# Three pairs of PSUM banks for the radial products of a graph convolution, and row numbers of the gather kept in SBUF

## The chip, the cores and the metric

The kernel runs on one core of a Trainium2 chip. The metric is the device time of one execution in microseconds (us), as the median of several runs. Lower is better. The engines are named as in the profile: PE is TensorE's matrix multiply and PEld its weight load, DVE is VectorE, ACT is ScalarE, POOL is GpSimd, SP is SyncE, which only issues DMAs here.

## The reference

A graph of 12,500 nodes with 32 features has 200,000 edges, sorted by destination. Twelve message-passing layers (the first network, `L0`) come first; the change doesn't touch them. Then comes one equivariant convolution (`L1`), and its output is added to the features:

```python
h = jnp.maximum(_layernorm(x, axis=-1), 0.0)
x = x + _L1_gnn_ref(h, edge_weight, edge_attr_3, edge_index, w1, b1, w2, b2)
```

For each edge the convolution computes a hidden layer of 64 values from one distance (`relu(d * w1 + b1)`), multiplies it with `w2` to radial weights, multiplies those with the source node's features and with spherical harmonics of the edge's direction (`einsum('euv,ef,evi,ofi->euo', Rb[..., k], Yf, Fb, C)`), and adds the 32 resulting values into the edge's destination node. The kernel folds the 320 radial weights per edge into 448 columns.

## The kernel before, in words

The edges have been sorted into slots: a tile is one slot for each of 125 lanes, a unit is 20 tiles (`UNIT_TILES`), and there are 100 units. Each slot has a record of 14 words in DRAM (`slots`): the number of the source row, the lane, the weight and the local frame. The convolution works in turns of two units, so in 50 turns (`UNIT_PAIRS`) of 40 tiles. A turn is cut into five groups of eight tiles (`PAIR_GROUPS`, `GROUP`), and a group into four pairs of tiles (`GROUP_PAIRS`). DVE does one `group_step` per group; I call it a step. A short loop behind the main one (the overflow turns, `Over`) does the same for the edges that found no slot, in three turns of three groups; there the sums of half tiles are added node by node.

All engines run in program order and meet through semaphores. The parts that matter:

- **PE**, `radial_pair` (L1893 to L1903): for each pair, two bias multiplications (L1898) and two fp32 ones (L1901) fill two PSUM banks, one per tile. Banks 0 to 3 make two pairs of banks (`radial = banks(0, QUAD)`). A pair may be filled when DVE has multiplied the pair before the last (`radial_used`), and when ACT has the hidden layer of its four tiles ready (`hidden_ready`). Behind the four pairs' products come 24 small matmuls (`add_group`, L1922), which add the group's messages into two more banks (`conv_sums`).
- **DVE**, `group_step` (L1356 on): `multiply` for pair 0 and 1 (L1347 and L1351 each read the pair's banks), `project` for the next group (three instructions at L1320, which need the gathered rows), `multiply` for pair 2, the reduction L1330, `multiply` for pair 3, `project_plus` (L1336), then reductions and products (L1376 to L1401) that end in the group's messages.
- **ACT**: `main_marks` (L1583, L1588), `main_small` (the hidden layer, L1567), `main_scalars` (L1605, eight features of each gathered row), in an order written out by hand (`pair_step`).
- **SP**: `load_rec` (L655) loads the records of half a turn, once DVE has signalled `unit_done` for the half (behind L1394 of group 2 and of group 4) and POOL `unit_claimed`.
- **POOL**: `gather_unit` (L766 on) waits for `unit_done` and for the records, then issues 20 indirect DMAs (L772), each of which gathers 125 rows of `feature_table` by the row numbers that stand in the records.

Before the graph layers, ten pieces of the records pass through SBUF (`pieces`), and DVE copies three of their columns out (L1076 to L1078); between them it waits for the next load.

Of the kernel before, what the change touches and what calls it, by code (L numbers as in the profile page):

```python
# [24 lines left out]
def build_gnn(nc, x, src, dst, edge_attr, edge_weight, lift_W, lift_b, proj_W, proj_b, w1, b1, w2, b2, out):  # L25
# [99 lines left out]
    assert PAIR_GROUPS * GROUP == 2 * UNIT_TILES and PAIR_GROUPS == 5  # L125
    BUFFER_OF = (0, 1, 0, 1, 2)
    CHUNK_PAIRS = STEPS // 2
    UNIT_PAIRS = UNITS // 2
# [33 lines left out]
    with ctx:  # L162
# [164 lines left out]
        spill_marks = carve(SPILL_RING * SPILL_BATCH * LANES // 2).bitcast(BF16).rearrange("p (t n) -> p t n", n=LANES)  # L327
        hgT = carve(2, BANK)
        lane_gap = message_words[:, 0:MARKED_BY_ACT * LANES // 2].bitcast(BF16).rearrange("p (t n) -> p t n", n=LANES)

# [50 lines left out]
        gathered_rows = hg_words[:, 1024:1024 + 2 * UNIT_TILES * D].rearrange("p (s t d) -> p s t d", s=2, d=D)  # L381
        rec_tiles = rec.rearrange("p s t w -> p (s t) w")
        row_tiles = gathered_rows.rearrange("p s t d -> p (s t) d")
        spill_dist = hgT[0:SPILL_PART, 0, 0:LANES]
# [21 lines left out]
        turned, outs = banks(4, 2), banks(0, 4)  # L406
        radial, conv_sums, half_sums = banks(0, QUAD), banks(4, 2), banks(4, 4)
        spill_dist_psum = psum[0:SPILL_PART, 7 * BANK + 256:7 * BANK + 256 + LANES]
# [99 lines left out]
        rec_loaded = [sem(f"rec_loaded{s}") for s in range(2)]  # L508
        unit_claimed = [sem(f"unit_claimed{s}") for s in range(2)]
        unit_done = [sem(f"unit_done{s}") for s in range(2)]  # L510
# [26 lines left out]
        def _(sp):  # L537
# [128 lines left out]
            with sp.Fori(0, UNIT_PAIRS, 1) as i:  # L666
                for half in range(2):
                    sp.wait_ge(unit_done[half], i + 1)
                    sp.wait_ge(unit_claimed[half], i + 1)
                    load_rec(half, i)  # L670
# [7 lines left out]
        def _(pool):  # L678
# [87 lines left out]
            def gather_unit(half, i):  # L766
                pool.wait_ge(features_stored, 16)
                pool.wait_ge(unit_done[half], i + 1)
                pool.wait_ge(rec_loaded[half], 16 * i + 16)
                claim(7 + half, unit_claimed[half])  # L770
                for t in range(UNIT_TILES):
                    g.indirect_dma_start(out=gathered_rows[0:SLOTS, half, t, :], out_offset=None, in_=feature_table,  # L772
                                         in_offset=bass.IndirectOffsetOnAxis(
                                             ap=rec[0:SLOTS, half, t, 0:1].bitcast(I32), axis=0)
                                         ).then_inc(rows_gathered[half * QUADS + t // QUAD], 16)
# [22 lines left out]
        def _(dve):  # L798
# [16 lines left out]
            for s in range(2):  # L815
                v.engine_nop().then_inc(unit_claimed[s], 1)
                v.engine_nop().then_inc(unit_done[s], 1)
# [255 lines left out]
            for k in range(PIECES):  # L1073
                at = slice(k * PIECE, (k + 1) * PIECE)
                dve.wait_ge(slots_loaded[k % 2], 16 * (k // 2) + 16)
                v.tensor_copy(slot_lane[0:SLOTS, at], pieces[0:SLOTS, k % 2, :, 1])  # L1076
                v.tensor_copy(slot_w[0:SLOTS, at], pieces[0:SLOTS, k % 2, :, 2])
                v.tensor_copy(slot_src[0:SLOTS, at], pieces[0:SLOTS, k % 2, :, 3]).then_inc(slots_read, 1)  # L1078
            dve.wait_ge(src_psum_ready, 1)
# [220 lines left out]
            class Main:  # L1300
                chain, groups, first_group, first_turn = conv_step, PAIR_GROUPS, 0, 0
                row_of, rec_of = row_tiles, rec_tiles

            class Over:
                chain, groups, first_group, first_turn = over_step, SPILL_GROUPS, MAIN_GROUPS, UNIT_PAIRS
                row_of, rec_of = spill_rows, spill_rec

            def frames_of(kind, g):
# [34 lines left out]
            def multiply(kind, nth, g, pair):  # L1343
                at, bank = slice(2 * pair, 2 * pair + 2), slice(2 * (pair % 2), 2 * (pair % 2) + 2)
                z = inputs_of(g)[:, at, :, :]
# [10 lines left out]
            def group_step(kind, i, g, ahead):  # L1356
# [16 lines left out]
                if ahead:  # L1373
                    plus = project_plus(kind, nxt, summed)
                dve.wait_ge(radial_used, GROUP_PAIRS * nth + GROUP_PAIRS + 2)
                vectors = chain.mark(v.tensor_reduce(  # L1376
# [94 lines left out]
        def _(act):  # L1471
# [127 lines left out]
            def main_scalars(i, g):  # L1599
# [77 lines left out]
        def _(pe):  # L1677
# [215 lines left out]

            def radial_pair(nth, slot, pair):
                pe.wait_ge(hidden_ready, nth + 1)
                pe.wait_ge(radial_used, 2 * nth + pair + 1)
                for odd in range(2):
                    mm(radial[:, 2 * pair + odd, 0:MIX_S + MIX_V], ones_bf[odd * HIDDEN:odd * HIDDEN + PARTS, :],  # L1898
                       bias_bf[odd * HIDDEN:odd * HIDDEN + PARTS, :], start=True, stop=False)
                for odd in range(2):  # L1900
                    last = mm(radial[:, 2 * pair + odd, 0:MIX_S + MIX_V],  # L1901
                              hidden[odd * HIDDEN:(odd + 1) * HIDDEN, slot, pair * LANES:(pair + 1) * LANES],
                              w2_mix[odd * HIDDEN:(odd + 1) * HIDDEN, :], start=False, stop=True)  # L1903
                last.then_inc(radial_ready, 1)

            def first_quad(group):
                for pair in range(2):
                    radial_pair(2 * group, 0, pair)

            def second_quad(group):  # L1910
                for pair in range(2):
                    radial_pair(2 * group + 1, 1, pair)

# [18 lines left out]

            first_quad(0)
            with pe.Fori(0, CHUNKS - 1, 1) as j:
                clear_conv_sums(j)
                with pe.Fori(0, CHUNK_PAIRS, 1) as m:
                    for g in range(PAIR_GROUPS):
                        nth = (j * CHUNK_PAIRS + m) * PAIR_GROUPS + g
                        second_quad(nth)
                        first_quad(nth + 1)  # L1940
                        add_group(nth, g)
            clear_conv_sums(CHUNKS - 1)
            with pe.Fori((CHUNKS - 1) * CHUNK_PAIRS, UNIT_PAIRS - 1, 1) as m:
                for g in range(PAIR_GROUPS):
                    second_quad(m * PAIR_GROUPS + g)
                    first_quad(m * PAIR_GROUPS + g + 1)
                    add_group(m * PAIR_GROUPS + g, g)
            for g in range(PAIR_GROUPS):
                nth = (UNIT_PAIRS - 1) * PAIR_GROUPS + g
                second_quad(nth)  # L1950
                if g + 1 < PAIR_GROUPS:
                    first_quad(nth + 1)
                add_group(nth, g)
# [14 lines left out]

            turns = pe.value_load(conv_turns[0:1, 0:1], min_val=1, max_val=MAX_SPILL_TURNS * SPILL_PARTS)
            with pe.Fori(0, turns, 1) as i:  # L1970
                pe.wait_ge(conv_loaded, 16 * i + 16)
                nc.tensor.transpose(spill_dist_psum, spill_rec[:, 0:SPILL_PART, 2], identity[:, :]
                                    ).then_inc(spill_turned_ready, 1)
                first_quad(i * SPILL_GROUPS + MAIN_GROUPS)
                for g in range(SPILL_GROUPS):
                    nth = i * SPILL_GROUPS + g + MAIN_GROUPS
                    second_quad(nth)
                    if g + 1 < SPILL_GROUPS:
                        first_quad(nth + 1)
                    add_over(nth, g)  # L1980
# [23 lines left out]
```

## Time and profile before

| | us |
|---|---|
| median of 3 runs | 11822.15 (11821.74 to 11833.75) |
| the profiled execution, its own time | 11825.35 |
| its span, first to last instruction | 11823.7 |
| start of the convolution's first step | 8035.76 |
| end of the 50 turns, the last chunk's sums begin to be moved | 11559.04 |
| mean granted TensorE clock | 0.791 |

Everything up to about 8000 us is the sorting and the twelve layers; from there to the end is the convolution. Times of the trace are counted from the span's start. An idle time in brackets stands before the instruction of its row, with the instruction whose end released it.

### The profile page before, as it was taken

How to read it: one execution, taken by the hardware profiler on the slowest of the kernel's cores; microseconds unless marked ns; L12 is line 12 of the kernel's file. 1: busy time of each engine (PE TensorE's matmuls, PEld its weight loads, DVE VectorE, ACT ScalarE, POOL GpSimd, SP SyncE). 2: the span in 40 equal slices, each digit the busy share in tenths (PEclk: the TensorE clock that was granted, in tenths of full speed). 3: DMA queues.
4: the chain of work that ended last, by engine and by line, in shares of the span. 5: the costliest groups of instructions: out<-in, count | busy, mean ns of one | idle time of the engine just before them, and what ended most of it. 6: DMA issues, size and time to landing. Idle time of an engine off the chain costs nothing.

```text
span 11823.7 us, 340699 instructions
## 1 busy us (share of the span) xinstructions
PE 7408.7 (63%) x130038; PEld 4971.8 (42%) x130039; DVE 9354.8 (79%) x19079; ACT 3124.7 (26%) x7571; POOL 5296.6 (45%) x5027
## 2 busy tenths in 40 slices
PE   2555555200877877777777787775666666666663
PEld 2444444100766666666666676661222222222221
DVE  8777777457777877777777777778999999999995
ACT  0111111057222222222222222223333333333331
POOL 3777777400321221231131122116667766676773
PEclk9999999965988988888898898885555555555555
DMA  4111111067745754654564575551111111111111
GB/s 168 26 25 26 26 25 26 27 233 272 205 146 148 208 150 150 177 166 148 163 189 148 161 208 162 160 151 37 34 32 33 32 31 34 32 33 32 31 32 19
DMA packets 718056, 1212.33 MB, mean 103 GB/s; under 512 B 186449, under 2 KB 334068, under 8 KB 713636
## 3 DMA queue, kind: packets, MB, share of 16 engines
q1 hardware_dynamic: 434084, 1058.42, 28.6%
q0 software_dynamic: 146832, 69.31, 5.7%
q10 hardware_dynamic: 136012, 67.95, 2.4%
q8 instruction: 907, 14.86, 0.5%
q14 instruction: 221, 1.80, 0.1%
HBM read 1050.89 MB, written 140.94 MB: 101 GB/s over the span
## 4 chain that ended last, share of the span: by engine, by line
PE 37%; DVE 18%; issue 18%; DMA 4%; POOL 3%; DVEq 1%; ACT 1%; SPq 0%; POOLq 0%; ACTq 0%
PE psum L1814 9%; PE psum L1782 9%; PE psum L1901 7%; PE psum L1797 6%; DVE space L1383 2%; DVE space L1351 2%; PE psum L1898 2%; DMA space<-src_rows 2%; POOL space L772 2%; PE psum L1859 2%; DVE space L1387 1%; PE psum L1886 1%; DVE space L1394 1%; DMA space<-slots 1%; PE psum L1870 1%
## 5 line engine op out<-in xcount | busy, mean ns | idle before, releaser
L772 POOL DMA_INDIRECT space<-feature_table,space x2000 | 2430.5, 1215 | 598.3 <-issue 587.9
L700 POOL TENSOR_TENSOR claim_out<-claim_in 128x1 f32<-128x1 f32 x443 | 108.3, 245 | 5072.1 <-DMA table<-space 2639.0
L1901 PE MATMUL psum<-w_mix,space 64*128 64x448 f32 x4144 | 1818.2, 974 | 0.0
L1532 ACT ACTIVATE space<-psum 128x375 f32<-128x375 f32 x2400 | 955.1, 436 | 3006.7 <-PE psum L1782 2963.9
L709 POOL DMA_INDIRECT slots<-space x1568 | 1506.7, 961 | 466.1 <-issue 412.8
L1137 DVE TENSOR_TENSOR space<-psum,space 128x320 f32<-128x320 f32 x2400 | 1069.0, 486 | 786.1 <-PE psum L1797 715.6
L1782 PE MATMUL psum<-space 128*32 128x125 fp8e4 x72000 | 1341.1, 224 | 255.8 <-issue 253.2
L1814 PE MATMUL psum<-space 128*128 128x96 bf16 x24000 | 1292.6, 207 | 235.4 <-issue 146.2
L1782 PEld LDWEIGHTS psum<-space 128*32 128x32 bf16 x72000 | 1079.2, 98 | 509.8 <-issue 504.5
L1814 PEld LDWEIGHTS psum<-space 128*128 128x128 fp8e4 x24000 | 1105.3, 97 | 391.3 <-issue 270.9
L755 POOL DMA_INDIRECT space<-table,space x864 | 1099.4, 1272 | 280.9 <-issue 280.9
L1143 DVE TENSOR_TENSOR space<-space 128x320 f32<-128x320 f32 x2400 | 1062.6, 485 | 35.7 <-issue 35.7
L1147 DVE TENSOR_TENSOR space<-space 128x320 f32<-128x320 f32 x2400 | 1069.5, 487 | 0.0
L1797 PE MATMUL psum<-identity,space 128*128 128x128 f32 x6000 | 906.6, 283 | 109.4 <-ACT space L1532 41.0
L1347 DVE TENSOR_TENSOR space<-psum,space 128x512 f32<-128x512 f32 x1036 | 711.9, 687 | 261.1 <-PE psum L1901 250.6
L1922 PE MATMUL psum<-space 128*128 128x32 bf16 x6000 | 200.4, 188 | 1090.9 <-DVE space L1401 1090.9
L1722 PE MATMUL psum<-space 128*128 128x100 bf16 x1568 | 295.3, 278 | 824.0 <-DVE space L942 688.8
L1922 PEld LDWEIGHTS psum<-space 128*128 128x128 bf16 x6000 | 180.8, 104 | 1369.6 <-issue 1336.5
L1797 PEld LDWEIGHTS psum<-identity,space 128*128 128x128 f32 x6000 | 655.0, 143 | 139.0 <-issue 79.4
L1583 ACT ACTIVATE space<-columns,space 128x128 bf16<-128x128 f32 x2072 | 656.1, 387 | 198.6 <-issue 178.2
L1567 ACT ACTIVATE space<-space,b_col,w_col 128x256 f32<-128x256 f32 x518 | 309.4, 598 | 1359.7 <-PE psum L1901 1350.2
L1898 PE MATMUL psum<-space,ones_bf 3*128 3x448 bf16 x2072 | 548.9, 527 | 187.9 <-DVE space L1351 112.6
(289 smaller groups left out, 11803.5 us busy)
## 6 DMA issues: line engine op xcount, KB each, us to landing
space<-marks SPq DMA_DIRECT2D x2400, 320.0 KB
space<-src_rows SPq DMA_DIRECT2D x102, 640.0 KB, 4.7
marks<-space SPq DMA_DIRECT2D x100, 640.0 KB, 3.2
space<-distances ACTq DMA_DIRECT2D x200, 320.0 KB, 4.8
space<-block_ids SPq DMA_DIRECT2D x198, 200.0 KB
slots<-space SPq DMA_DIRECT2D x83, 448.0 KB, 9.1
space<-feature_table,space POOLq DMA_INDIRECT x2072, 2.7
slots<-space POOLq DMA_INDIRECT x1608, 2.1
```

Source lines behind the costliest of these rows:

```text
L709: g.indirect_dma_start(out=slots, out_offset=bass.IndirectOffsetOnAxis(ap=stage_row[:, s, c:c + 1], axis=0), in_=stage[:, s, c, :], in_off ...
L755: g.indirect_dma_start(out=spill_rows[0:GATHERED, t, :], out_offset=None, in_=table, in_offset=bass.IndirectOffsetOnAxis(ap=spill_rec[0:GA ...
L772: g.indirect_dma_start(out=gathered_rows[0:SLOTS, half, t, :], out_offset=None, in_=feature_table, in_offset=bass.IndirectOffsetOnAxis(ap= ...
L1137: v.tensor_tensor(row[:, half, :], slots_of_unit[:, half, :], slot_w[:, bass.ds(at * UNIT_TILES + k * HALF_TILES, HALF_TILES)].rearrange(" ...
L1143: v.tensor_tensor(left[:, half, :], row[:, half, :], tops[0][:, half, :], ALU.subtract).then_inc(left_split, 1)
L1147: v.tensor_tensor(least[:, half, :], left[:, half, :], tops[1][:, half, :], ALU.subtract).then_inc(least_split, 1)
L1532: a.activation(to[:, s0:s1, :, :], pair_picked[:, bank, 0:(s1 - s0) * PICK_COLS].rearrange("p (k c r) -> p k c r", k=s1 - s0, r=CAP), ACT.Copy
L1782: last = mm(pair_picked[D * g:D * (g + 1), bank, (s - s0) * PICK_COLS:(s - s0 + 1) * PICK_COLS], parts[:, q * SRC_PER_TILE + s, c, :], cel ...
L1797: last = nc.tensor.transpose(slots_of_unit[:, c * LANE_GROUPS:(c + 1) * LANE_GROUPS, :].rearrange("p t d -> p (t d)"), picked[:, q % 2, c, ...
L1814: last = mm(unit_sums[:, t // SUMS_PER_BANK, to:to + PARTS * D], mark_ring[:, q % RING, 1, t * LANES:(t + 1) * LANES], message_halves[:, q ...
L1898: mm(radial[:, 2 * pair + odd, 0:MIX_S + MIX_V], ones_bf[odd * HIDDEN:odd * HIDDEN + PARTS, :], bias_bf[odd * HIDDEN:odd * HIDDEN + PARTS, ...
L1901: last = mm(radial[:, 2 * pair + odd, 0:MIX_S + MIX_V], hidden[odd * HIDDEN:(odd + 1) * HIDDEN, slot, pair * LANES:(pair + 1) * LANES], w2 ...
```

## The change

The radial products get three pairs of banks (0 to 5) and the message sums move to banks 6 and 7. Pair number n of a turn (0 to 19) uses the banks n mod 3. PE now fills pair 3 of a group and then pairs 0, 1 and 2 of the next, before it adds the group. In the overflow turns two pairs are used in the old order, and PE's first transposition there waits until the sums have been moved.

The row numbers are copied out of the pieces early (a fourth DVE copy for each of ten pieces, into `slot_row`). During the convolution ACT copies 20 of them per half turn into `row_index` (`copy_index`), and the gathers read them there. They wait for that copy and for a new signal, `rows_projected`, which DVE gives in step 1 and in step 3 when the last reader of the half's rows has run, and no longer for `unit_done` and the records. SP's load of records no longer waits for POOL.

```diff
+    TURN_PAIRS = PAIR_GROUPS * GROUP_PAIRS
+    RADIAL_PAIRS = 3
...
+        slot_row = carve(SLOT_TILES).bitcast(I32)
...
+        row_index = hg_words[:, 1024 + 2 * UNIT_TILES * D:1024 + 2 * UNIT_TILES * (D + 1)].bitcast(I32).rearrange(
+            "p (s t) -> p s t", s=2)
...
-        radial, conv_sums, half_sums = banks(0, QUAD), banks(4, 2), banks(4, 4)
+        radial, conv_sums, half_sums = banks(0, 2 * RADIAL_PAIRS), banks(6, 2), banks(4, 4)
...
                     sp.wait_ge(unit_done[half], i + 1)
-                    sp.wait_ge(unit_claimed[half], i + 1)
                     load_rec(half, i)
...
             def gather_unit(half, i):
                 pool.wait_ge(features_stored, 16)
-                pool.wait_ge(unit_done[half], i + 1)
-                pool.wait_ge(rec_loaded[half], 16 * i + 16)
-                claim(7 + half, unit_claimed[half])
+                pool.wait_ge(index_copied, 2 * i + half + 1)
+                pool.wait_ge(rows_projected, 2 * i + half + 1)
+                pool.wait_ge(scatter_claimed[half], i + TURNS // 2)
+                claim(7 + half, scatter_claimed[half])
...
-                                             ap=rec[0:SLOTS, half, t, 0:1].bitcast(I32), axis=0)
+                                             ap=row_index[0:SLOTS, half, t:t + 1], axis=0)
...
+                v.tensor_copy(slot_row[0:SLOTS, at], pieces.bitcast(I32)[0:SLOTS, k % 2, :, 0])
...
+                def ring_of(g, pair):
+                    return (g * GROUP_PAIRS + pair) % RADIAL_PAIRS
...
             def multiply(kind, nth, g, pair):
-                at, bank = slice(2 * pair, 2 * pair + 2), slice(2 * (pair % 2), 2 * (pair % 2) + 2)
+                at, ring = slice(2 * pair, 2 * pair + 2), kind.ring_of(g, pair)
+                bank = slice(2 * ring, 2 * ring + 2)
...
                     plus = project_plus(kind, nxt, summed)
+                if ahead and kind is Main and nxt in (2, 4):
+                    v.engine_nop().then_inc(rows_projected, 1)
...
+            def copy_index(i, half):
+                if not (isinstance(i, int) and i == 0):
+                    act.wait_ge(rows_gathered[(half + 1) * QUADS - 1], 16 * QUAD * i)
+                    act.wait_ge(scalars_copied, PAIR_GROUPS * i - 2 + 2 * half)
+                a.activation(row_index[0:SLOTS, half, :],
+                             slot_row[0:SLOTS, bass.ds((2 * i + half) * UNIT_TILES, UNIT_TILES)],
+                             ACT.Copy).then_inc(index_copied, 1)
...
+                    if q8 in (2, 6) and not last:
+                        copy_index(i + 1, q8 // 4)
...
+            act.wait_ge(rec_cleared, 4)
+            for half in range(2):
+                copy_index(0, half)
...
-            def radial_pair(nth, slot, pair):
-                pe.wait_ge(hidden_ready, nth + 1)
-                pe.wait_ge(radial_used, 2 * nth + pair + 1)
+            def radial_pair(group, pair, ring, held):
+                slot, upper = divmod(pair, 2)
+                pe.wait_ge(hidden_ready, 2 * group + slot + 1)
+                pe.wait_ge(radial_used, GROUP_PAIRS * group + pair + 3 - held)
...
+            def main_pair(group, g, pair):
+                at = (g * GROUP_PAIRS + pair) % TURN_PAIRS
+                radial_pair(group, pair, at % RADIAL_PAIRS, 2 if at < 2 else RADIAL_PAIRS)
+
+            def over_pair(group, pair):
+                radial_pair(group, pair, pair % 2, 2)
...
                         nth = (j * CHUNK_PAIRS + m) * PAIR_GROUPS + g
-                        second_quad(nth)
-                        first_quad(nth + 1)
+                        main_pair(nth, g, 3)
+                        for pair in range(3):
+                            main_pair(nth + 1, g + 1, pair)
                         add_group(nth, g)
...
             turns = pe.value_load(conv_turns[0:1, 0:1], min_val=1, max_val=MAX_SPILL_TURNS * SPILL_PARTS)
+            pe.wait_ge(sums_moved, CHUNKS + 1)
```

## Rows read from the trace of the kernel before

**Rows 1.** The page: busy time of each engine; DVE's busy tenths in 40 slices.
```profile
PE 7408.7 (63%) x130038; PEld 4971.8 (42%) x130039; DVE 9354.8 (79%) x19079; ACT 3124.7 (26%) x7571; POOL 5296.6 (45%) x5027
...
DVE  8777777457777877777777777778999999999995
```

**Rows 2.** Busy by stretch: length, PE, PEld, DVE, ACT, POOL, TensorE clock, DMA, GB/s.
```profile
9000.00:9600.00 600.00, 404.44 (x2042) 129.92 (x2040) 545.80 (x982) 222.06 (x552) 421.95 (x361) 0.57 0.19 32
```

**Rows 3.** Waits of DVE, 8035 to 11558 us: total, times, longest.
```profile
DVE space L1347 <- PE psum L1901: 228.1, 448, 1.5
DVE space L1320 <- DMA space<-feature_table,space: 35.8, 50, 7.0
DVE space L1347 <- issue: 8.0, 38, 0.3
```

**Rows 4.** DVE in one step, in order of time: start, length, instruction, idle before.
```profile
9321.45 0.68 DVE L1347 TENSOR_TENSOR space<-psum,space 128x512 f32<-128x512 f32 x1
...
9323.58 0.88 DVE L1320 TENSOR_TENSOR space<-space 128x192 f32<-128x192 f32 x3
...
9325.05 0.69 DVE L1347 TENSOR_TENSOR space<-psum,space 128x512 f32<-128x512 f32 x1 [0.59 <-PE psum L1901]
...
9326.13 0.74 DVE L1330 TENSOR_REDUCE space<-space 128x192 f32<-128x576 f32 x1
...
9327.33 0.69 DVE L1347 TENSOR_TENSOR space<-psum,space 128x512 f32<-128x512 f32 x1 [0.46 <-PE psum L1901]
...
9328.54 1.74 DVE L1376 TENSOR_REDUCE space<-space 128x192 f32<-128x1536 f32 x1
...
9335.39 0.68 DVE L1347 TENSOR_TENSOR space<-psum,space 128x512 f32<-128x512 f32 x1
```

**Rows 5.** DVE in the first turn, a pair 3 whose products were there.
```profile
8046.89 0.74 DVE L1330 TENSOR_REDUCE space<-space 128x192 f32<-128x576 f32 x1
8047.55 0.68 DVE L1347 TENSOR_TENSOR space<-psum,space 128x512 f32<-128x512 f32 x1
```

**Rows 6.** PE in the step of rows 4, in order of time.
```profile
9321.68 0.80 PE L1922 MATMUL psum<-space 128*128 128x32 bf16 x24 [5.04 <-DVE space L1401]
...
9322.66 0.55 PE L1898 MATMUL psum<-space,ones_bf 3*128 3x448 bf16 x2 [0.17 <-DVE space L1351]
...
9323.14 1.86 PE L1901 MATMUL psum<-w_mix,space 64*128 64x448 f32 x4
...
9324.94 0.55 PE L1898 MATMUL psum<-space,ones_bf 3*128 3x448 bf16 x2
```

**Rows 7.** POOL by line, 8100 to 11500 us: busy, mean ns, idle before.
```profile
L772 POOL DMA_INDIRECT space<-feature_table,space x1937 | 2353.5, 1215 | 579.4 <-issue 569.1 <-DMA space<-slots 10.4
L700 POOL TENSOR_TENSOR claim_out<-claim_in 128x1 f32<-128x1 f32 x97 | 23.0, 237 | 446.6 <-DMA space<-slots 445.3
```

**Rows 8.** The convolution's start in order of time; last the store's time to landing.
```profile
8005.16 0.33 SPq L659 DMA_DIRECT2D feature_table<-space  x1
...
8014.23 0.85 SPq L655 DMA_DIRECT2D space<-slots  x2
...
8019.57 1.21 POOL L772 DMA_INDIRECT space<-feature_table,space  x1 [0.17 <-issue]
...
8031.62 1.20 POOL L772 DMA_INDIRECT space<-feature_table,space  x1 [0.30 <-issue]
...
8032.85 0.93 DVE L1320 TENSOR_TENSOR space<-space 128x192 f32<-128x192 f32 x3 [21.22 <-DMA space<-feature_table,space]
...
feature_table<-space SPq DMA_DIRECT2D x1, 1664.0 KB, 5.3
```

**Rows 9.** DVE between the pieces of the records, one of eight such waits.
```profile
2374.69 0.33 DVE L1076 COPY space<-space 125x200 f32<-125x200 f32 x1 [9.67 <-DMA space<-slots]
```

**Rows 10.** The first overflow turn's start: PE's transposition and ACT's copy.
```profile
11559.29 0.39 PE L1972 MATMUL psum<-identity,space 128*24 128x128 f32 x1 [0.29 <-issue]
...
11560.10 0.27 ACT L1636 ACTIVATE space<-psum 24x128 f32<-24x128 f32 x1 [21.55 <-DVE xs L1413]
```

More of the change, by code:

```diff
@@ L508, in build_gnn @@
         rec_loaded = [sem(f"rec_loaded{s}") for s in range(2)]
-        unit_claimed = [sem(f"unit_claimed{s}") for s in range(2)]
+        index_copied = sem("index_copied")
+        rows_projected = sem("rows_projected")
         unit_done = [sem(f"unit_done{s}") for s in range(2)]
@@ L815, in _ @@
             for s in range(2):
-                v.engine_nop().then_inc(unit_claimed[s], 1)
+                v.engine_nop().then_inc(rows_projected, 1)
                 v.engine_nop().then_inc(unit_done[s], 1)
@@ L1306, in _, with ring_of @@
                 row_of, rec_of = spill_rows, spill_rec
+                def ring_of(g, pair):
+                    return pair % 2
             def frames_of(kind, g):
@@ L1374, in group_step @@
                     plus = project_plus(kind, nxt, summed)
+                if ahead and kind is Main and nxt in (2, 4):
+                    v.engine_nop().then_inc(rows_projected, 1)
                 dve.wait_ge(radial_used, GROUP_PAIRS * nth + GROUP_PAIRS + 2)
@@ L1892, in _ @@
             pe.wait_ge(weights_spread, 16 * 3)
-            def radial_pair(nth, slot, pair):
-                pe.wait_ge(hidden_ready, nth + 1)
-                pe.wait_ge(radial_used, 2 * nth + pair + 1)
+            def radial_pair(group, pair, ring, held):
+                slot, upper = divmod(pair, 2)
+                pe.wait_ge(hidden_ready, 2 * group + slot + 1)
+                pe.wait_ge(radial_used, GROUP_PAIRS * group + pair + 3 - held)
                 for odd in range(2):
-                    mm(radial[:, 2 * pair + odd, 0:MIX_S + MIX_V], ones_bf[odd * HIDDEN:odd * HIDDEN + PARTS, :],
+                    mm(radial[:, 2 * ring + odd, 0:MIX_S + MIX_V], ones_bf[odd * HIDDEN:odd * HIDDEN + PARTS, :],
                        bias_bf[odd * HIDDEN:odd * HIDDEN + PARTS, :], start=True, stop=False)
                 for odd in range(2):
-                    last = mm(radial[:, 2 * pair + odd, 0:MIX_S + MIX_V],
-                              hidden[odd * HIDDEN:(odd + 1) * HIDDEN, slot, pair * LANES:(pair + 1) * LANES],
+                    last = mm(radial[:, 2 * ring + odd, 0:MIX_S + MIX_V],
+                              hidden[odd * HIDDEN:(odd + 1) * HIDDEN, slot, upper * LANES:(upper + 1) * LANES],
                               w2_mix[odd * HIDDEN:(odd + 1) * HIDDEN, :], start=False, stop=True)
                 last.then_inc(radial_ready, 1)
[L1906 to L1912, printed above, removed]
+            def main_pair(group, g, pair):
[3 more added lines that the diff above has]
+                radial_pair(group, pair, pair % 2, 2)
             def add_group(nth, g):
@@ L1931, in clear_conv_sums @@
                        start=True, stop=True)
-            first_quad(0)
+            for pair in range(3):
+                main_pair(0, 0, pair)
             with pe.Fori(0, CHUNKS - 1, 1) as j:
@@ L1938, in _ @@
                         nth = (j * CHUNK_PAIRS + m) * PAIR_GROUPS + g
-                        second_quad(nth)
-                        first_quad(nth + 1)
+                        main_pair(nth, g, 3)
+                        for pair in range(3):
+                            main_pair(nth + 1, g + 1, pair)
                         add_group(nth, g)
@@ L1944, in _ @@
                 for g in range(PAIR_GROUPS):
-                    second_quad(m * PAIR_GROUPS + g)
-                    first_quad(m * PAIR_GROUPS + g + 1)
-                    add_group(m * PAIR_GROUPS + g, g)
+                    nth = m * PAIR_GROUPS + g
+                    main_pair(nth, g, 3)
+                    for pair in range(3):
+                        main_pair(nth + 1, g + 1, pair)
+                    add_group(nth, g)
             for g in range(PAIR_GROUPS):
                 nth = (UNIT_PAIRS - 1) * PAIR_GROUPS + g
-                second_quad(nth)
+                main_pair(nth, g, 3)
                 if g + 1 < PAIR_GROUPS:
-                    first_quad(nth + 1)
+                    for pair in range(3):
+                        main_pair(nth + 1, g + 1, pair)
                 add_group(nth, g)
@@ L1973, in _ @@
                                     ).then_inc(spill_turned_ready, 1)
-                first_quad(i * SPILL_GROUPS + MAIN_GROUPS)
+                for pair in range(2):
+                    over_pair(i * SPILL_GROUPS + MAIN_GROUPS, pair)
                 for g in range(SPILL_GROUPS):
                     nth = i * SPILL_GROUPS + g + MAIN_GROUPS
-                    second_quad(nth)
+                    for pair in range(2, GROUP_PAIRS):
+                        over_pair(nth, pair)
                     if g + 1 < SPILL_GROUPS:
-                        first_quad(nth + 1)
+                        for pair in range(2):
+                            over_pair(nth + 1, pair)
                     add_over(nth, g)
```

## The prediction

> **What bounds the kernel now.** I began with the page. No engine fills the span, and the page's table in 40 slices shows that the share of the whole says little: DVE's digit is mostly 7 in the layers and 9 in the slices of the convolution [rows 1]. The table by stretches gives the number for 600 us in its middle: DVE works 545.80 of 600 us, POOL 422, PE 404, ACT 222, and the granted TensorE clock is 0.57 of full, near the lower of its two levels, 1.2 GHz [rows 2]. So the most that a change of waiting can win there is DVE's remaining 9%. I then asked who DVE waits for in the 50 turns: 228.1 us in 448 waits for radial products, 35.8 us in 50 waits for gathered rows, 8.0 us at the edges of its own loop [rows 3]. The last column of that view matters too: one of the 50 waits for rows is 7.0 us long, so the other 49 have 28.8 us, 0.59 each.
>
> Then one step in order of time [rows 4]. It lasts from 9321.45 to 9335.39, 13.94 us. Pairs 0 and 1 run without a gap; DVE then projects, waits 0.59 us for pair 2 and 0.46 us for pair 3. The same stretch on PE [rows 6] shows the reason: PE starts pair 2 at 9322.66, when DVE's L1351 on pair 0 has just ended, and needs 9324.94 - 9322.66 = 2.28 us for a pair; DVE goes on at 9325.05, 2.39 us after PE's start. There are two pairs of banks, so this wait is for a bank, not for PE's throughput: four pairs and the additions are 4 x 2.28 + 0.80 = 9.9 us of a 13.94 us step. Nine waits in a turn of ten products is right too: the wait for rows, once a turn, covers one.
>
> **The products.** With three pairs of banks, pair 2 is filled in the step before. Pair 3 starts when pair 0 is used, at about 1.2 us into the step (today's 9322.66 - 9321.45), and is ready at 1.21 + 2.39 = 3.6 us. DVE wants it without any wait at 9327.33 - 9321.45 - 0.59 - 0.46 less two overlaps (below), 4.7 us. That is 1.1 us of slack. The next group's pairs 0 to 2 follow on PE at about 5.9, 8.2 and 10.5 us, and DVE wants them at 12.7 us and later; at a turn's edge, where the ring of three restarts, pair 0 waits for pair 2's use and the chain ends near 11.1 us. The additions come behind them and wait for the messages, as now. ACT's hidden layer for the later pairs is released by pair 3's products at 3.6 us and takes 0.6 us, so it is there before PE comes to it. Thus both waits go.
>
> A wait costs more than its length, since neighbours on DVE overlap. After L1330, which takes 0.74 us, pair 3 starts 0.66 us later where its products are there [rows 5] and 1.20 us later where they aren't [rows 4]: 0.54 us gained for a wait of 0.46. So the products give 228.1 + 448 x 0.08 = 263.9 us. The step becomes 13.94 - 1.05 - 0.16 = 12.73 us, and a turn, now (11559.04 - 8035.76) / 50 = 70.5 us with its loop edge and its share of the moved sums, loses 5.3 us.
>
> **The gathers.** POOL needs 1.215 us and 0.299 us of idle (579.4 over 1937) for one gather [rows 7], 1.514 us, so 40 x 1.514 + 0.5 us for its two claims = 61.1 us a turn. It stands idle 445.3 us in 48 turns, about 9 us each, for records [rows 7]: half 0 isn't asked for before step 2 has ended, though its last reader runs early in step 1. After the change the request comes when `project_plus` of step 1 has run, some 7 us into it, and no longer with the end of step 2 and a load behind it: the rest of step 1 (5.7), step 2 (12.7) and the load, 5.3 us from its issue to the first gather at the start [rows 8], make it about 23 us earlier. Then half 0's gathers run from 7 to 38 us behind the start of step 1, half 1's (asked for at 32) from 38 to 68, and the next turn's request comes at 71: POOL has 64.5 - 61.1 = 3.4 us a turn to spare (64.5 is 70.5 less the 5.9 us a turn that both parts give) and DVE finds every group's rows some 20 us early. So the 49 short waits go, 28.8 + 49 x 0.08 = 32.7 us. Without this part the same waits would have grown, since DVE's two steps between request and use get 2.4 us shorter.
>
> Here a page speaks against the change, and the trace first. While the first eight gathers are issued DVE stands still, and they take 12.05 us, from 8019.57 to the ninth's start at 8031.62: 1.506 us each [rows 8]; with DVE 91% busy it is 1.514 us [rows 2, 7]. DVE's work costs POOL 0.5%. The Trainium skill (SBUF — State Buffer, Who interferes with whom) says that a DVE instruction with two SBUF inputs contends with a GpSimd instruction that reads SBUF, and that the later one blocks fully. L1320 and four other lines of the step have two SBUF inputs, so by that rule a fuller DVE holds POOL more; by the rows it hardly can. The sum goes by the rows; the rule is the mechanism behind the last rival.
>
> **The start.** The gathers now begin when the table is stored and ACT has copied the row numbers. The store is issued at 8005.16, takes 0.33 us to issue and 5.3 us to land: about 8010.8, against 8019.57 behind the record load that is issued at 8014.23 [rows 8]. ACT's copies are short and stand before its first DMAs. The first eight rows then bring the first projection from 8032.85 to about 8024.1, 8.8 us earlier; the records (8019) and the first pair's products (8024) are just there. The 7.0 us wait for group 1 stays, as POOL still needs 12.1 us for eight gathers. Bounds: 0, if the store lands as late as the records, and 8.8. I take 8.8, by the landing time in the row.
>
> **What is added.** Two `engine_nop` a turn behind `project_plus`, 100 in all; no row shows one. Below: nothing, when it hides behind L1376's wait for the last product; above: the 0.21 us that a loop's edge costs DVE [rows 3], 21 us. I take 0.05 us, 5 us, since the instruction behind it starts 1.21 us after pair 3 anyhow and waits for that product's end. ACT's 100 small copies lie on an engine with 378 of 600 us free [rows 2], and what they wait for, its own scalars and rows that have landed, has been waited for in the same place already. Ten more DVE copies before the layers: eight lie behind a transfer that takes 10.4 us per piece (9.67 of them waiting) [rows 9], as the next load is already under way; about 0.25 us at the first and at the last stay, 0.5 us, at most 2.5 if none hides. The first overflow turn: PE's transposition of 0.39 us moves behind the moving of sums, for which ACT's copy waits today [rows 10]: 0.6 us later, on the path. The overflow turns are otherwise as before.
>
> **The sum.** 263.9 + 32.7 + 8.8 - 5 - 0.5 - 0.6 = 299.3 us. Against the profiled execution's own 11825.35 that is 11526; that execution lies 3.2 us (0.03%) above the median, so I predict 11523 us, 2.5% faster. In this kernel 0.2%, 24 us, is about what can be told from no change.
>
> **Rivals.**
> *A wait for products stays.* Pair 3 still needs pair 0's bank in the same step, and its slack is 1.1 us. If PE comes to it that much later (the additions before it, the bias loads, a semaphore's way), pair 3's wait remains at its present size: 250 x 0.54 = 135 us less, 11658. For it: the slack is a sum of small terms. Against: PE's row shows it starting within 0.1 us of DVE's release. 12%.
> *Banks were not the cause.* If the hidden layer on ACT decides when PE starts, a third pair is filled no earlier, and only 32.7 + 8.8 us less 6 are won: 11787. Against it stands the release by L1351 in rows 6. 3%.
> *POOL becomes the bound, and the kernel slower.* POOL's place is `gather_unit`, 40 gathers a turn. If a DVE without pauses stretches a gather, POOL decides from (64.5 - 0.5) / 40 = 1.60 us on, 6% above today's 1.514. With every 0.05 us beyond it the turn is 2 us longer, 100 us in all. At (70.5 - 0.5) / 40 = 1.75 us the turn is as long as today's and the kernel is slower from there; at 1.9 us it would be 76.5 us, 6 us more in each of 50 turns, and 12122 us in all. For it: the shared port of the rule above. Against: the 0.5% between idle and busy. 3% for slower, 7% for the stretch between, about 11600.
>
> **How the numbers follow.** The forecast has 73%, pair 3's wait 12%, POOL as a bound that still leaves a gain 7%, banks not the cause 3%, POOL slower 3%, and 2% for no change at all by a mixture that I can't name. The range must leave out at most two in ten. Downward it holds the free nops and a little more overlap (11505); upward the full price of the nops, the copies and a start that isn't won (16 + 2 + 9 us give 11550), and it reaches into the milder cases of the two rivals in between: 11505 to 11590. Faster by over 0.2%: 95%; within: 2%; slower: 3%.
>
> **What would show it.** After the change the waits of DVE's L1347 for L1901 should be under 20 us in the turns, the step 12.7 us and the turn 64.5 us. L1320's wait for rows should appear once or twice only. POOL's waits should no longer name the records, its idle time before a claim be near 3.4 us a turn, and a gather still take 1.51 us. DVE should be busy near 99% of a middle stretch. The first projection should start near 8024. The prediction fails if PE's pair 3 ends later than 4.7 us into a step, if DVE's own instructions get longer than in rows 4, or if a gather takes more than 1.60 us.

## The result, and the profile after

The changed kernel takes 11488.53 us (median of 4 runs, 11477.02 to 11492.08) against 11827.95 us of the kernel before on the same chip (median of 4, 11821.74 to 11861.58): the ratio is 0.9706, with a 95% interval of 0.9686 to 0.9726. The forecast was 11523 us in a range from 11505 to 11590. The kernel became faster, as forecast, but the time lies below the range. The profiled executions took 11491.44 us (span 11489.8) and 11825.35 us (span 11823.7): 333.9 us between them, where the sum had 299.3, 35 us less.

The page of the changed kernel, busy time of each engine and DVE's tenths in 40 slices, as in [rows 1]:

```profile
PE 7439.1 (65%) x130026; PEld 4989.4 (43%) x130039; DVE 9304.2 (81%) x19089; ACT 3129.3 (27%) x7671; POOL 5310.8 (46%) x5027
...
DVE  8777777547878777777777777877999999999995
```

The stretch in the middle of the convolution, as in [rows 2]:

```profile
9000.00:9600.00 600.00, 439.52 (x2248) 141.75 (x2250) 588.72 (x1078) 244.72 (x626) 462.55 (x393) 0.59 0.21 36
```

DVE's waits from 8008 to 11232 us, which are the 50 turns, as in [rows 3]:

```profile
DVE space L1361 <- issue: 8.7, 39, 0.3
DVE space L1333 <- DMA space<-feature_table,space: 5.9, 1, 5.9
...
DVE space L1361 <- PE psum L1931: 0.4, 1, 0.4
```

L1361 is the former L1347, L1333 the former L1320, L1931 the former L1901. Of 228.1 us for products 0.4 are left, of 50 waits for rows the one in the first turn. DVE is busy 98% of the stretch, from 91%. One step on DVE shows the same, with no brackets at all; compare the second, fourth and fifth of these rows with [rows 4] and [rows 5]:

```profile
9313.72 0.68 DVE L1361 TENSOR_TENSOR space<-psum,space 128x512 f32<-128x512 f32 x1
...
9315.84 0.89 DVE L1333 TENSOR_TENSOR space<-space 128x192 f32<-128x192 f32 x3
9316.65 0.68 DVE L1361 TENSOR_TENSOR space<-psum,space 128x512 f32<-128x512 f32 x1
...
9317.71 0.74 DVE L1343 TENSOR_REDUCE space<-space 128x192 f32<-128x576 f32 x1
9318.37 0.68 DVE L1361 TENSOR_TENSOR space<-psum,space 128x512 f32<-128x512 f32 x1
...
9326.43 0.68 DVE L1361 TENSOR_TENSOR space<-psum,space 128x512 f32<-128x512 f32 x1
```

The step is 9326.43 - 9313.72 = 12.71 us; the prediction had 12.73. PE in the same step, as in [rows 6]:

```profile
9313.95 0.80 PE L1951 MATMUL psum<-space 128*128 128x32 bf16 x24 [2.54 <-DVE space L1417]
9314.92 0.55 PE L1928 MATMUL psum<-space,ones_bf 3*128 3x448 bf16 x2 [0.17 <-DVE space L1365]
...
9317.20 0.55 PE L1928 MATMUL psum<-space,ones_bf 3*128 3x448 bf16 x2
```

Pair 3 starts 1.20 us into the step, released by DVE's use of pair 0. With the 2.39 us from PE's start to DVE's that [rows 4] and [rows 6] gave, it is ready at 9317.31, and DVE takes it at 9318.37: the slack is 1.06 us where 1.1 was expected. POOL from 8200 to 11100 us, as in [rows 7]:

```profile
L778 POOL DMA_INDIRECT space<-feature_table,space x1816 | 2234.2, 1230 | 559.5 <-issue 559.2 <-DVEq L1390 0.3
L705 POOL TENSOR_TENSOR claim_out<-claim_in 128x1 f32<-128x1 f32 x91 | 18.3, 201 | 89.0 <-DVEq L1390 87.7
```

POOL no longer waits for records. What it waits for now is DVE's signal at L1390, 89.0 us in 45.5 turns, 2.0 a turn (3.4 were expected). A gather takes (2234.2 + 559.5) / 1816 = 1.538 us, 0.024 us longer than before. The start, as in [rows 8]:

```profile
7985.10 0.33 SPq L665 DMA_DIRECT2D feature_table<-space  x1
...
7990.71 0.49 POOL L705 TENSOR_TENSOR claim_out<-claim_in 128x1 f32<-128x1 f32 x1 [192.96 <-DMA feature_table<-space]
...
7991.47 1.21 POOL L778 DMA_INDIRECT space<-feature_table,space  x1 [0.26 <-issue]
...
8006.06 0.90 DVE L1333 TENSOR_TENSOR space<-space 128x192 f32<-128x192 f32 x3 [14.49 <-DMA space<-feature_table,space]
```

POOL is released 5.6 us after the store's issue, as counted, and starts gathering 0.8 us later for its claim.

**Where the time went.** The part of the trace that the prediction had left alone shows the rest. These rows are the last normalisation ahead of the first layer and of the convolution. In the kernel before:

```profile
2941.12 1.89 DVE L1227 CAST space<-space 128x3328 bf16<-128x3328 f32 x1
...
8003.24 1.89 DVE L1124 TENSOR_SCALAR space<-space 128x3328 f32<-128x3328 f32 x1
```

and in the changed one:

```profile
2945.20 1.89 DVE L1234 CAST space<-space 128x3328 bf16<-128x3328 f32 x1
...
7983.18 1.89 DVE L1131 TENSOR_SCALAR space<-space 128x3328 f32<-128x3328 f32 x1
```

The twelve layers, which the change doesn't touch, take 5062.1 us before and 5038.0 us after. Cut at these rows, at the first product (8035.76 and 8008.93), at the moving of the last sums (11559.04 and 11226.18) and at the span's end, the difference of 333.9 us between the two traces is:

| stretch | before | after | gained | predicted |
|---|---|---|---|---|
| up to the layers | 2941.1 | 2945.2 | -4.1 | -0.5 |
| layers | 5062.1 | 5038.0 | 24.1 | 0 |
| to the first product | 32.5 | 25.8 | 6.8 | 8.8 |
| 50 turns | 3523.3 | 3217.3 | 306.0 | 291.6 (263.9 + 32.7 - 5) |
| overflow turns | 264.7 | 263.6 | 1.0 | -0.6 |

DVE's waits in the layers give a hint. First the kernel before (2941 to 8004 us), then the changed one (2945 to 7984 us):

```profile
DVE space L1137 <- PE psum L1797: 715.6, 542, 6.4
...
DVE space L1137 <- issue: 38.1, 20, 3.8
DVE space L1143 <- issue: 35.7, 24, 2.4
```

```profile
DVE space L1144 <- PE psum L1826: 767.7, 583, 7.8
...
DVE space L1144 <- issue: 1.5, 9, 0.2
```

"Issue" is idle time in which the profile shows nothing that the engine waits for. DVE had 73.8 us of it in the layers, in pieces of up to 3.8 us, and has 1.5 us now; 52.1 us of that came back as waits for PE (715.6 to 767.7). One more row differs where it shouldn't, that of the instruction packets on queue 14, before and after:

```profile
q14 instruction: 221, 1.80, 0.1%
```

```profile
q14 instruction: 100, 0.82, 0.0%
```

Of 1.80 MB in 221 packets, 8 KB each, 121 packets are no longer fetched. In the stretch of the layers alone they are, before and after:

```profile
q14 instruction: 204, 1.67, 0.1%
```

```profile
q14 instruction: 84, 0.69, 0.0%
```

That is 17 for each layer, and 7 after. The idle time and the packets meet in the trace too. These are DVE's rows in the first layer of the kernel before, and queue 14 from 3153.10 to 3156.90, which is the first of the two gaps:

```profile
3150.76 2.35 DVE L1154 TENSOR_REDUCE space<-psum 128x480 f32 x4
3156.92 0.89 DVE L1137 TENSOR_TENSOR space<-psum,space 128x320 f32<-128x320 f32 x2 [3.82 <-issue]
3160.18 0.89 DVE L1143 TENSOR_TENSOR space<-space 128x320 f32<-128x320 f32 x2 [2.36 <-issue]
```

```profile
q14 instruction: 2, 0.02, 2.2%
```

Of the 38 pauses of at least 0.5 us that "issue" has in the layers, 31 (62.4 of 72.7 us) have a packet of queue 14 in them or in the 0.7 us ahead of them. My theory from here: DVE fetched part of the code of its loop over chunks again and again and stood idle for it, and ten added copies ahead of the loop moved the loop to where it fits. The rivals are the chance of one execution, and something that the copies themselves do.

### The profile page after: what moved, and what is told of

Read it like the earlier page. It is cut to its first block, busy times and chain, and to the rows that moved or that the text cites. A ratio compares the mean times of both kernels' runs of the same rounds, so it can differ in the third digit from the quotient of the medians.

```text
span 11489.8 us, 341188 instructions
## 1 busy us (share of the span) xinstructions
PE 7439.1 (65%) x130026; PEld 4989.4 (43%) x130039; DVE 9304.2 (81%) x19089; ACT 3129.3 (27%) x7671; POOL 5310.8 (46%) x5027
## 4 chain that ended last, share of the span: by engine, by line
PE 30%; DVE 26%; issue 17%; DMA 3%; POOL 2%; DVEq 1%; ACT 1%; SPq 0%; POOLq 0%; ACTq 0%
PE psum L1843 10%; PE psum L1811 10%; PE psum L1826 6%; DVE space L1365 3%; DVE space L1398 2%; DVE space L1399 2%; DMA space<-src_rows 2%; DVE space L1361 2%; DVE space L1333 2%; PE psum L1888 2%; PE psum L1915 2%; DVE space L1410 2%; DVE space L1403 2%; DVE space L1343 2%; POOL space L778 1%
## 5 line engine op out<-in xcount | busy, mean ns | idle before, releaser
L778 POOL DMA_INDIRECT space<-feature_table,space x2000 | 2462.6, 1231 | 615.1 <-issue 614.8
L1931 PE MATMUL psum<-w_mix,space 64*128 64x448 f32 x4144 | 1838.8, 984 | 0.0
L1144 DVE TENSOR_TENSOR space<-psum,space 128x320 f32<-128x320 f32 x2400 | 1066.0, 485 | 786.8 <-PE psum L1826 767.7
L1361 DVE TENSOR_TENSOR space<-psum,space 128x512 f32<-128x512 f32 x1036 | 704.6, 680 | 32.0 <-PE psum L1931 21.3
L1931 PEld LDWEIGHTS psum<-w_mix,space 64*128 64x128 f32 x4144 | 502.2, 295 | 378.7 <-issue 378.7
```

The costliest lines, as they stand in the source:

```text
L1144: v.tensor_tensor(row[:, half, :], slots_of_unit[:, half, :], slot_w[:, bass.ds(at * UNIT_TILES + k * HALF_TILES, HALF_TILES)].rearrange(" ...
L1361: v.tensor_tensor(prod_s[:, at, :, :], radial[:, bank, 0:MIX_S].rearrange("p t (u j) -> p t u j", j=2 * U), z[:, :, 0:2, :].rearrange("p t ...
L1931: last = mm(radial[:, 2 * ring + odd, 0:MIX_S + MIX_V], hidden[odd * HIDDEN:(odd + 1) * HIDDEN, slot, upper * LANES:(upper + 1) * LANES], ...
```

## The experiments

Ten runs of eight kernels follow, on three chips. On one of them, the slow chip (`copies_only`, `pad10`, `banks_only` and `rows_only`), the kernel before takes 13092.55 us, 10% more. Nearly all of it lies in the sorting and the layers, but the turns are longer too: 3540.3 and 3539.2 us in `copies_only` and `pad10`, which leave them as they are, against 3523.3. Ratios are always to the kernel before on the same chip; the kernel before has no trace on these three, so stretches are compared with those of a padded kernel on the same chip.

**Only the copies.** The kernel before with the one part of the change that runs ahead of the layers, the ten DVE copies; nobody reads their result.

```diff
+        slot_row = carve(SLOT_TILES).bitcast(I32)
...
+                v.tensor_copy(slot_row[0:SLOTS, at], pieces.bitcast(I32)[0:SLOTS, k % 2, :, 0])
```

> The kernel before with nothing but the ten DVE copies of row numbers ahead of the layers (their result is not used). Theory (place of DVE's code): with ten more instructions in front, DVE's loop over the chunks no longer waits for its own code: idle 'issue' before L1137 and L1143 falls from 74 us to under 5, about 120 fewer instruction packets of 8 KB on queue 14, layers 20 us shorter, whole kernel 17 us faster, about 11805. Rival (chance of the clock or of the run): issue idle stays at 74 us, time 2.5 us longer than before.

Measured: 13076.21 us against 13092.55, 0.9986 (0.9976 to 0.9997), so 16 us by the medians. Queue 14:

```profile
q14 instruction: 110, 0.90, 0.0%
```

The packets went as expected, 84 of them are left in the layers. The idle time did not go: 37.4 us stay before L1139, where under 5 were expected.

**Only ten no-operations.**

```diff
+            for _ in range(10):
+                v.engine_nop()
             for k in range(PIECES):
```

> The kernel before with ten DVE engine no-operations ahead of the piece copies and nothing else. Place of DVE's code: as copies_only, layers 20 us shorter, about 11802. Rival (something the copies themselves do, or chance): no change from before, 11822.

Measured: 13075.08 us, 0.9986 (0.9974 to 0.9998), 111 packets. So ten instructions that do nothing do what the copies do, and the copies' data has no part in it. Here too "issue" stayed in part (54.6 us before L1139, none before L1145). What stayed is something else: none of the 16 pauses of at least 0.5 us that these two traces have left (5.5 to 7.8 us long, but for a few) has a packet of queue 14 in it. `banks_only`, whose loop lies as in the kernel before, has 107.7 us of "issue" in its layers on this chip. So I repeated `pad10` on a chip like that of the result:

> The ten no-operations once more, on another chip than the first time, which was 10% slower in the sorting and the layers. Place of DVE's code: 111 packets on queue 14, idle 'issue' before L1139 and L1145 in the layers under 5 us in place of 74, and 0.2 to 0.5% faster than before, as the changed kernel against its variant with ACT's copies (52 us). Rival: under 0.1%.

Measured: 11794.67 us against 11852.85, 0.9952 (0.9939 to 0.9966): 58 us, from ten no-operations. DVE's waits in its layers, 2940 to 7972 us:

```profile
DVE space L1139 <- PE psum L1799: 763.2, 590, 6.4
...
DVE space L1139 <- issue: 1.2, 7, 0.2
```

The layers take 5028.0 us there, with 84 packets in them, and the turns 3523.4, as before. In `banks_again`, on the same chip and with 204 packets, the layers take 5062.8 us: 34.8 of the 58 us are found there.

**128 and five no-operations.** The same edit with other numbers.

> The kernel before with 128 DVE no-operations ahead of the piece copies: exactly one 8 KB packet of code more, if an instruction takes 64 bytes. If what counts is where the chunk loop lies against the packets, 128 puts it back where it was: about 221 packets on queue 14 and idle 'issue' in the layers, as before. If any added code helps: about 110.

> The kernel before with five DVE no-operations in the same place. The step from 220 to 110 packets lies somewhere between 0 and 10 added instructions; half of the padding shows on which side of 5. No forecast beyond that the number is one of the two.

Measured, first 128, then five:

```profile
q14 instruction: 221, 1.81, 0.1%
```

```profile
q14 instruction: 230, 1.88, 0.0%
```

128 added instructions are much like none: 221 packets and 57.2 + 29.8 = 87.0 us of "issue" in the layers. Five have more idle time than none (130.4 us of it), ten have next to none. So it isn't the amount of added code that counts, but where it puts the loop. In the layers both kernels have the same 204 packets as the kernel before; the ten more of `pad5` lie in the overflow turns (14 against 4). The number of packets therefore doesn't set the idle time: the kernel before has 38 pauses (of at least 0.5 us) of 1.9 us on average, `pad5` 25 of 5.0 us. Each of the two ran once (11853.89 and 11870.11 us against a median of 11855.67), and only their packets and idle time are read.

**The changed kernel with DVE's code in its old place.** ACT makes the ten copies; two more waits of SP keep them safe.

```diff
-                v.tensor_copy(slot_row[0:SLOTS, at], pieces.bitcast(I32)[0:SLOTS, k % 2, :, 0])
...
+            for k in range(PIECES):
+                at = slice(k * PIECE, (k + 1) * PIECE)
+                act.wait_ge(slots_loaded[k % 2], 16 * (k // 2) + 16)
+                a.activation(slot_row[0:SLOTS, at], pieces.bitcast(I32)[0:SLOTS, k % 2, :, 0], ACT.Copy
+                             ).then_inc(rows_read, 1)
```

> The changed kernel with the ten copies of row numbers made by ACT in place of DVE, so that DVE's code ahead of the layers has the length it has in the kernel before. Place of DVE's code: the packets on queue 14 go back from 100 to about 210 and the idle 'issue' before the layers' L1144 and L1150 comes back; 15 to 20 us slower than the changed kernel, turns unchanged at 3217 us. Rival (the 20 us were chance, or came from the copies): within 5 us of the changed kernel.

It ran beside the changed kernel as it is:

> The changed kernel once more, as the control for the next run on the same chip and against the kernel before on this chip. If the turns, the start and the code's place are the whole of it, the turns are 3217 us long again (306 us shorter), with no wait for products or rows in them after the first, and DVE's code queue carries 100 packets. The layers depend on the chip and aren't forecast.

Measured: the control 11487.0 us, 0.9683 (0.9665 to 0.9702); with ACT's copies 11538.83 us, 0.9730 (0.9713 to 0.9747), both against 11855.67 us. The turns are 3218.6 and 3219.3 us long. The variant's DVE waits in the layers, 2954 to 8050 us, and its queue 14:

```profile
DVE space L1146 <- issue: 50.7, 25, 5.5
...
DVE space L1152 <- issue: 33.7, 24, 2.1
```

```profile
q14 instruction: 230, 1.88, 0.1%
```

In the layers these are again 204 packets, against 84 of the control; I had expected 210 in all, and the ten more than in the kernel before lie in the overflow turns. So DVE's code at its old length brings the layers' packets and the idle time back. Between the medians lie 52 us, more than the 15 to 20 that I expected. The two traces are 68.3 us apart, as the variant's is its slowest run: 59.7 of them in the layers (5095.3 and 5035.6) and 9.0 ahead of the layers, which may belong to ACT's copies and SP's waits as well as to the place. What is left of the gain without the place of DVE's code, 317 us by the medians, agrees with the 314 us of the table's last three rows.

**Only the banks.** All hunks of the change on `radial`, `multiply` and PE; records and gathers as before.

```diff
-        radial, conv_sums, half_sums = banks(0, QUAD), banks(4, 2), banks(4, 4)
+        radial, conv_sums, half_sums = banks(0, 2 * RADIAL_PAIRS), banks(6, 2), banks(4, 4)
...
-                        second_quad(nth)
-                        first_quad(nth + 1)
+                        main_pair(nth, g, 3)
+                        for pair in range(3):
+                            main_pair(nth + 1, g + 1, pair)
```

> Only the three pairs of banks; gathers and records as before. Theory: pair 2's and pair 3's waits go (264 us), but DVE now comes to the next turn's first rows 1.2 us earlier and waits there 1.9 us a turn in place of 0.6 (63 us more), so about 200 us faster than before, near 11620, L1320's successor waiting some 90 us for rows in the turns. The layers keep their 74 us of DVE idle under 'issue'. Rival (the parts add up as the prediction's sum has them): 264 us faster, 11560, row waits near 36 us.

> Only the banks, on another chip than the first time. The turns are again 3350 us long, 173 us shorter than before, with some 117 us of waits for rows and none for products; the layers as before. About 1.45% faster.

Measured: 0.9856 (0.9838 to 0.9875) on the slow chip, with 116.9 us of waits for rows in the turns where about 90 were expected; 11666.61 us against 11852.85, 0.9844 (0.9831 to 0.9858), on the other. The turns take 3344.0 us there, 179.4 less than in `pad10_again` on the same chip. The wait for rows has grown; these are one turn's from the second run, of 0.59 us before, and its total with the 21.1 us of the start:

```profile
9307.47 0.90 DVE L1328 TENSOR_TENSOR space<-space 128x192 f32<-128x192 f32 x3 [2.21 <-DMA space<-feature_table,space]
9320.95 0.95 DVE L1328 TENSOR_TENSOR space<-space 128x192 f32<-128x192 f32 x3 [0.25 <-DMA space<-feature_table,space]
```

```profile
DVE space L1328 <- DMA space<-feature_table,space: 143.4, 89, 21.1
```

In the turns that is 122.3 us, where it was 35.8.

**Only the rows.** All other hunks.

```diff
-                pool.wait_ge(unit_done[half], i + 1)
-                pool.wait_ge(rec_loaded[half], 16 * i + 16)
+                pool.wait_ge(index_copied, 2 * i + half + 1)
+                pool.wait_ge(rows_projected, 2 * i + half + 1)
```

> Only the row numbers in SBUF and the earlier gathers; two pairs of banks. Theory: the wait for rows of 0.59 us a turn covers pair 2's wait of 0.59 us in the same step, so its removal uncovers that one: 500 waits for products in the turns in place of 448, about 252 us, and the turns are within 5 us of before. The start gives 6.7 us. If DVE's code layout is what made the layers faster, another 17 us from them: about 11798; if that was chance, 11815. Rival (additive parts): 33 us more from the turns, 11765 or 11782.

Measured: 13050.29 us, 0.9976 (0.9959 to 0.9992), 31 us by the ratio and 42 by the medians. The turns take 3528.8 us, 10 to 12 less than in `pad10` and `copies_only` on the same chip; I had expected them within 5 us of before. DVE waits there, 9202 to 12730 us:

```profile
DVE space L1352 <- PE psum L1921: 250.5, 429, 1.5
...
DVE space L1325 <- DMA space<-feature_table,space: 7.0, 1, 7.0
```

The waits for rows are gone but for the first, and those for products have grown to 250.5 us, from 200.9 in `pad10` on this chip and 228.1 in the kernel before on its own. Besides those 10 to 12 us, what is gained is the start (24.5 us in place of 32.2 in `pad10`) and the place of the code (100 packets).

## Why the prediction was wrong in size

**What bounds the kernel, and the products: right.** The wait was for a bank. PE still starts pair 3 at DVE's release, its slack is 1.06 us, and the step is 12.71 us. The rivals "a wait for products stays" and "banks were not the cause" are refuted by 0.4 us of such waits in the turns, and the second by the 179 us of the banks alone.

**The turns: right, a little undersized.** Each of the 497 removed waits gave its length and 0.08 us of overlap in the sum. Measured, 306.0 us less 1.1 (the first turn's wait for rows is shorter) less 256.9 of waits leaves 48.0 us, 0.097 each: 8 us more. The two no-operations a turn cost nothing that shows: L1349 and L1392 behind it start 0.13 to 0.14 us apart with and without one. That is 5 us more.

**The gathers: right.** They run ahead, no row is waited for after the first turn, and POOL has 2.0 us a turn to spare in place of 3.4; a gather got 1.6% longer (1.538 us; 1.532 and 1.527 in `after_same` and `after_act`) while DVE went from 91 to 98% busy. The rival in which POOL becomes the bound needed 6%. The Trainium skill (SBUF — State Buffer, Who interferes with whom) says that a DVE instruction with two SBUF inputs contends with a GpSimd instruction that reads SBUF. The direction agrees, but the runs don't show that this is the reason: in `rows_only` a gather takes 1.529 us, against 1.518 in `pad10` on the same chip, with DVE 91% busy in both. So a part of the rise comes with the rows part of the change and not with a busier DVE. (The prediction counted five lines of a step with two SBUF inputs; in the code there are eight, which changes no number of it.)

**The parts don't add up alone.** Banks alone give 179 us in the turns and rows alone 10 to 12, each against a kernel on the same chip; both give 306. The prediction said that without the second part the waits for rows would grow; it didn't price that, and its 32.7 us for the gathers reads as if it were their own. It isn't: the step with the wait for rows had no wait for pair 2. Each part uncovers the other's wait, and some 115 us belong to the pair of them (an estimate, as the three numbers come from three chips).

**The start: right in kind, oversized.** It gave 6.8 us in place of 8.8. POOL's start was hit but for its claim (0.8), and the eighth gather's rows took 1.3 us longer from issue to DVE (8002.01 to 8006.06; before, 8030.11 to 8032.85), which I didn't pursue.

**The step that failed is "what is added".** The prediction took the ten DVE copies for 0.5 us, nearly all hidden behind a transfer, and put their effect on everything behind them at nothing, without a reason. Their own cost is small: the pieces take 94.9 us in the changed kernel's first trace, 92.6 in its second, and 92.1 before. But they move all of DVE's later code. The loop over the chunks then no longer fetches ten packets a layer, and the layers get 24.1 us shorter in the pair of profiles, 34.8 us between `banks_again` and `pad10_again`, and 59.7 us between `after_act` and its control. Where the prediction had nothing for the layers, 24.1 us were gained; in its other terms the turns gave 14 us more, the overflow turns 2 more, the start 2 less and the stretch ahead of the layers 4 less: 299 + 24 + 14 + 2 - 2 - 4 = 333 us. Without the layers' 24.1 us the measured difference is 309.8 us, a time of 11512 us and inside the range. The range was built from the bounds of the terms that I had, and this one wasn't among them: its effect lies in a stretch that the diff doesn't touch, and its sign is open until the lengths are counted.

The Trainium skill has this rule (Runtime: NRT & Kernel Launch, Instruction fetch mechanics): a taken branch to a target outside the two blocks that an engine holds forces a fetch before execution goes on. The page has blocks of 16 KiB; the packets here are of 8 KB. The traces agree in kind: with 204 packets in the layers there are 74 to 130 us of idle "issue", with 84 at most 1.7 us, and on the slow chip 107.7 us with 204 and 37 to 55 us with 84, in pauses that have no packet in them. Which branch left which block isn't visible in them. I had read the row of queue 14 on the page before and passed over it; 38.1 and 35.7 us of "issue" before L1137 and L1143 also stood in the page's groups.

What stays open is why the layers' length varies as much as it does with the same packets: five traces with 204 of them in the layers have 5062 (the kernel before), 5063 (`banks_again`), 5074 (`pad128`), 5095 (`after_act`) and 5108 us (`pad5`), three with 84 have 5028 to 5038 us. The idle time goes along only roughly (73.8, 85.6, 87.0, 84.4 and 130.4 us for the five). On the slow chip single traces show no clear gain in the layers (5816.0, 5796.8 and 5769.0 us with 84 packets, 5807.4 with 204), and the medians one of 16 to 17 us. Nor was it tried how long the loop is in instructions, so I can't say beforehand which paddings are good.

## What to carry to other kernels

Two waits that cover each other must be removed together, and the gain of each alone says little: look which waits a step would have if the largest weren't there. Instructions added ahead of a loop in an engine's program move that loop; where the trace has idle "issue" time inside a loop and packets of the instruction queue fall into it, the place of that loop may be worth tens of microseconds, as here, and a few no-operations ahead of it are a cheap experiment. When a difference is to be explained, cut both traces at the same instructions first, in the stretches that the change doesn't touch too, and compare stretches only between runs on the same chip.

## What the runs showed of the hardware that I had not expected

Adding 0, 5, 10 and 128 no-operations ahead of DVE's loops gave 221, 230, 110 and 221 instruction packets of 8 KB, of them 204, 204, 84 and 204 in the layers, and, on chips of like speed, 74, 130, 1.2 and 87 us of idle "issue" there. The same program took 13092.55 us on one chip and 11827.95 to 11855.67 us on three others. Little of the difference is in the convolution: with DVE's work as in the kernel before, its turns took 3539 to 3540 us there and 3522 to 3523 elsewhere.
